# Local attention in a woven one-core kernel: first-pass exponentials kept and transposed, instead of scores and exponentials computed a second time

## What is computed

```python
sim = jnp.einsum('bhwid,bhwjd->bhwij', bq, bk)      # bq scaled by 8; keys: own window and the one before
mask = (i < j) | (i > j + WINDOW) | (j == -1)
sim = jnp.where(mask, -jnp.finfo(sim.dtype).max, sim)
attn = jax.nn.softmax(sim, axis=-1)
out = jnp.einsum('bhwij,bhwjd->bhwid', attn, bv)
```

## Time and profile before

| | |
|---|---|
| median of 3 runs | 2591.12 us (2587.27 to 2595.66) |
| the profiled execution | 2581.11 us |
| its span, first to last instruction | 2579.3 us |
| mean granted TensorE clock | 0.866 |
| instructions | 53778 |

### The profile page before, as it was taken

One profiled execution on the slowest core, in us unless ns is written; L12 is line 12 of the kernel. 1 busy time (PEld: TensorE's weight loads), 2 busy tenths in 40 slices (PEclk: granted clock), 3 DMA queues, 4 the chain that ended last, 5 costly groups with the idle time before them and its releaser, 6 DMA issues.

```text
span 2579.3 us, 53778 instructions
## 1 busy us (share of the span) xinstructions
PE 1943.3 (75%) x22054; PEld 1184.7 (46%) x22054; DVE 1351.0 (52%) x3132; ACT 1387.3 (54%) x3607; POOL 553.8 (21%) x613
## 2 busy tenths in 40 slices
PE   4239656888769777888779786888778876977777
PEld 3014344546444554446444454446444544456444
DVE  5133446554554737464654647374655556473553
ACT  1154525764476616763476527673476537672534
POOL 2710205030221105030312004030413023110230
PEclk9659867998889978998789878998799878997999
DMA  9203360002000100002000201002100201000000
GB/s 275 61 3 94 102 165 13 3 1 51 10 10 2 38 15 17 3 1 51 13 6 2 50 10 9 3 1 51 18 3 1 51 10 10 2 8 13 1 1 5
DMA packets 129890, 76.26 MB, mean 30 GB/s; under 512 B 76082, under 2 KB 121610, under 8 KB 127596
## 3 DMA queue, kind: packets, MB, share of 16 engines
q1 hardware_dynamic: 125548, 66.51, 10.6%
q0 software_dynamic: 4096, 6.32, 2.0%
HBM read 41.71 MB, written 33.16 MB: 29 GB/s over the span
## 4 chain that ended last, share of the span: by engine, by line
PE 38%; issue 23%; DVE 15%; ACT 12%; POOL 6%; another core or an unknown queue 3%; SPq 2%; DMA 1%; DVEq 0%; POOLq 0%; ACTq 0%
PE PS L1292 4%; PE PS L1433 4%; PE PS L596 3%; POOL area_b L1740 2%; DVE work_a L975 2%; PE PS L488 2%; ACT work_a L814 2%; PE PS L1325 2%; PE PS L1444 2%; PE PS L752 2%; PE PS L568 2%; DVE area_b L1625 2%; PE PS L1402 2%; PE PS L1364 1%
## 5 line engine op out<-in xcount | busy, mean ns | idle before, releaser
L1740 POOL TENSOR_TENSOR area_b<-area_b,tables 128x256 f32<-128x256 f32 x256 | 213.0, 852 | 761.7 <-DVE area_b L1625 761.7
L797 ACT ACTIVATE work_a<-PS,work_a 128x512 bf16<-128x512 f32 (+3 forms) x512 | 265.2, 543 | 132.7 <-DVE work_a L924 119.9
L924 DVE TENSOR_REDUCE work_a<-PS 128x2 f32<-128x1024 f32 (+3 forms) x256 | 201.4, 820 | 148.1 <-PE PS L488 86.5
L488 PE MATMUL PS<-strip,pick 64*128 64x128 bf16 (+4 forms) x2560 | 250.7, 277 | 0.0
L1529 ACT ACTIVATE area_b<-PS,neg_max 128x192 f32<-128x192 f32 (+1 forms) x512 | 202.3, 421 | 75.9 <-DVE neg_max L1665 58.6
L814 ACT ACTIVATE work_a<-PS 128x1024 f32<-128x1024 f32 (+1 forms) x192 | 169.4, 882 | 113.4 <-PE PS L488 112.9
L1292 PE MATMUL PS<-wqkv,area_b 128*128 128x512 f32 x384 | 201.9, 659 | 9.1 <-DVE area_b L1625 8.7
L534 PE MATMUL PS<-work_a 64*128 64x512 bf16 (+3 forms) x512 | 77.7, 345 | 159.1 <-ACT work_a L797 119.5
L1325 PE MATMUL PS<-area_b 64*128 64x192 f32 (+1 forms) x1024 | 141.6, 405 | 68.8 <-ACT area_b L1529 53.8
L596 PE MATMUL PS<-work_a 128*64 128x512 f32 (+3 forms) x1024 | 188.9, 471 | 4.0 <-ACT work_a L814 4.0
L1754 POOL TENSOR_TENSOR rstd_b<-var_eps_b,minus_half 128x4 f32<-128x4 f32 x16 | 16.4, 1025 | 786.5 <-DVE var_eps_b L120 786.5
(11 more groups left out here) (310 smaller groups left out, 4107.5 us busy)
## 6 DMA issues: line engine op xcount, KB each, us to landing
work_a<-stack_d SPq DMA_DIRECT2D x32, 512.0 KB
stack_d<-area_b SPq DMA_DIRECT2D x48, 192.0 KB, 3.3
stack_d<-area_b SPq DMA_DIRECT2D x32, 128.0 KB, 2.7
area_b<-in_L_attn_x_dram SPq DMA_DIRECT2D x4, 512.0 KB, 6.4
slots_in<-work_a SPq DMA_DIRECT2D x8, 256.0 KB, 4.9
stack_d<-work_a SPq DMA_DIRECT2D x4, 512.0 KB, 7.3
work_a<-xnT_d SPq DMA_DIRECT2D x8, 256.0 KB
work_a<-in_L_attn_x_dram SPq DMA_DIRECT2D x8, 256.0 KB
```

What stands on the lines that cost most here:

```text
L488: return nc.tensor.matmul(to, pick16[half_rows(e), half * P:(half + 1) * P], rows, start=False, stop=True, tile_position=(64 * e, 0), skip ...
L797: nc.scalar.activation(dump0[:, n % 2 * T:n % 2 * T + (i + 1) * P], PS[:, a:a + (i + 1) * P], ACT.Exp, bias=neg_max0[:, k:k + 1], accum_ou ...
L924: nc.vector.reduce_max(neg_max0[:, 2 * g * NT + i:(2 * g + 2) * NT:NT], at[:, :, Q_AT[i]:Q_AT[i] + (i + 1) * P], AX_X, negate=True).then_i ...
L1740: nc.gpsimd.tensor_tensor(to[:, n, :, r, :], src[:, n, :, 1 - r, :], table(2 * n + 1, t)[:, 32 * r:32 * r + 32].unsqueeze(1).to_broadcast( ...
```

## The change

It keeps the exponentials of the first pass in `work_b`, 896 columns for each head. DVE divides by the sums (`shared_out`: one reciprocal of 4 columns and four in-place products with a scalar for each partition, for each slot; slot m - 2 is handled behind the maximum of slot m, the last two at the first slot of the second pass). In the second pass PE transposes these blocks (8 f32 transposes of 128x128 in an even slot, 6 in an odd one), ACT copies them out with a plain copy of the same size as the former exponential, and the product with the values stays. The first 64 keys of a block that belong to the previous tile are taken with 64 columns of zeros before them; POOL writes these zeros (8 x 3 x 64 = 1536 columns) once for each layer, after waiting for the last `turned_q` and `turned_k`. PE's second pass waits for that and, for each pair of heads, for the products. Logarithms, shifts, their transposes and copies, the constant `select16` and the second pass of scores, masks and exponentials go. `probs2T` and the context now lie in `q2` and `k2`.

```diff
@@ -245,20 +243,16 @@
-probs2 = work_b[:, 0:2 * 768]
-dump2 = work_b[:, 2 * QK:3 * QK]
-ctx2T = rot
+probs2T = q2[:, 0:2 * 768]
+ctx2T = k2
...
-shiftT2 = sb("shiftT2", 2 * T, BF16)
...
-log_sums2 = sb("log_sums2", H2 * NT)
-shift_rest2 = sb("shift_rest2", NT * H2)
-shift_part2 = sb("shift_part2", NT * H2, BF16)
+inv_sums2 = sb("inv_sums2", H2 * NT)
@@ -446,6 +439,21 @@
+def probs_of(h, i):
+    a = h * 896 + (0, 192, 448, 704)[i]
+    return work_b[:, a:a + Q2_KEYS[i]]
...
+def own_keys_of(h, i):
+    return probs_of(h, i)[:, Q2_KEYS[i] - P:]
...
+def late_keys_of(h, i):
+    a = h * 896 + 256 * i - P
+    return work_b[:, a:a + P]
...
+zeros_of_probs2 = work_b.rearrange("p (h c) -> p h c", c=896)[:, :, P:].rearrange(
+    "p h (i c) -> p h i c", c=256)[:, :, :, 0:64]
@@ -1303,13 +1311,6 @@
-def shifts_T(half, k):
-    pe.wait_ge(s["shift_parts"], past("shift_parts", 3 * half + 3))
-    for i in range(NT):
-        a = (half * NT + i) * P
-        last = nc.tensor.transpose(bank(k, i * P, (i + 1) * P), shift_parts2[:, a:a + P], ident)
-    last.then_inc(s["shiftT"], 1)
@@ -1340,49 +1341,31 @@
     if m == 0:
-        fill(4)
+        fill(7)
         pe.wait_ge(s["sum"], past("sum", 28))
-        shifts_T(0, 4)
-        fill(3)
-        pe.wait_ge(s["shiftT_copied"], past("shiftT_copied", 1))
+        pe.wait_ge(s["zeroed"], past("zeroed", 1))
     else:
         pe.wait_ge(s["probs"], past("probs", m))
-    if m == 4:
-        pe.wait_ge(s["shiftT_copied"], past("shiftT_copied", 2))
-    half = g // 2
-    for j in (2 * x, 2 * x + 1):
-        n = K2_QUERIES[j]
-        for e in range(2):
-            h = 2 * g + e
+    pe.wait_ge(s["shared"], past("shared", 8 * g + 8))
+    for e in range(2):
+        for j in (2 * x, 2 * x + 1):
             a = (4 + e) * BANK + K2_AT[j]
-            nc.tensor.matmul(PS[:, a:a + n], select16[half_rows(e), (h % HH) * P:(h % HH + 1) * P],
-                             shiftT2[half_rows(e), half * T + j * P:half * T + j * P + n],
-                             start=(j % 2 == 0), stop=False, tile_position=(64 * e, 0),
-                             skip_group_check=True)
-        for e in range(2):
+            if j + 1 < NT:
+                nc.tensor.transpose(PS[:, a + P:a + 2 * P], late_keys_of(2 * g + e, j + 1), ident)
+            if j % 2:
+                nc.tensor.transpose(PS[:, a:a + P], own_keys_of(2 * g + e, j), ident)
+        for j in (2 * x, 2 * x + 1):
             a = (4 + e) * BANK + K2_AT[j]
-            nc.tensor.matmul(PS[:, a:a + n], k2[half_rows(e), g * T + j * P:g * T + (j + 1) * P],
-                             q2[half_rows(e), g * T + j * P:g * T + j * P + n], start=False, stop=False,
-                             tile_position=(64 * e, 0), skip_group_check=True)
-    for late in range(2):
-        for e in range(2):
-            to = bank(4 + e, 0, W2K[x])
-            if x:
-                last = limits(late, e, to, (2, 1)[late], 5)
-            else:
-                last = limits(late, e, to.rearrange("p (n c) -> p n c", c=KX), (2, 4)[late], 3, 2)
-    last.then_inc(s["scoresT"], 1)
+            if j % 2 == 0:
+                last = nc.tensor.transpose(PS[:, a:a + P], own_keys_of(2 * g + e, j), ident)
+    last.then_inc(s["flipped"], 1)
 if m == 1:
     pe.wait_ge(s["sum"], past("sum", 32))
-    shifts_T(1, 7)
 if m:
...
     pe.wait_ge(s["probs"], past("probs", m))
-    if x == 0:
-        if g == 1:
-            pe.wait_ge(s["shiftT_copied"], past("shiftT_copied", 2))
-        if g >= 2:
-            pe.wait_ge(s["ctxT"], past("ctxT", g - 1))
+    if x == 0 and g >= 2:
+        pe.wait_ge(s["ctxT"], past("ctxT", g - 1))
     for j in (2 * x, 2 * x + 1):
@@ -1390,7 +1373,7 @@
-last = nc.tensor.matmul(PS[r:r + D2, o:o + n], v2[:, v:v + D2], probs2[:, a:a + n],
+last = nc.tensor.matmul(PS[r:r + D2, o:o + n], v2[:, v:v + D2], probs2T[:, a:a + n],
@@ -1505,48 +1488,27 @@
-def shift_logs(half):
-    at = slice(half * NT * HH, (half + 1) * NT * HH)
-    act.wait_ge(s["sum"], past("sum", NT * HH * (half + 1)))
-    nc.scalar.activation(log_sums2[:, at], sums2[:, at], ACT.Ln).then_inc(s["log"], 1)
...
-def shifts_copied(half, k):
-    act.wait_ge(s["shiftT"], past("shiftT", half + 1))
-    nc.scalar.copy(shiftT2[:, half * T:(half + 1) * T], bank(k)).then_inc(s["shiftT_copied"], 1)
...
-n = 0
 for m in range(8):
     g, x = divmod(m, 2)
-    if m == 7:
-        shifts_copied(0, 4)
     act.wait_ge(s["max"], past("max", 3 * g + (2, 3)[x]))
...
             a, w = (4 + 2 * x + e) * BANK + Q2_AT[i], Q2_KEYS[i]
-            if n >= 4:
-                act.wait_ge(s["sum"], past("sum", n - 3))
-            nc.scalar.activation(dump2[:, n % 4 * 256:n % 4 * 256 + w], PS[:, a:a + w], ACT.Exp,
+            nc.scalar.activation(probs_of(2 * g + e, i), PS[:, a:a + w], ACT.Exp,
                                  bias=neg_max2[:, k:k + 1], accum_out=sums2[:, k:k + 1]
                                  ).then_inc(s["sum"], 1)
-            n += 1
-    if m == 3:
-        shift_logs(0)
-    if m == 7:
-        shift_logs(1)
     yield
...
         x = m % 2
-        act.wait_ge(s["scoresT"], past("scoresT", m + 1))
+        act.wait_ge(s["flipped"], past("flipped", m + 1))
         if m >= 2:
...
         a = 768 * (m % 2)
-        nc.scalar.activation(probs2[:, a:a + 2 * W2K[x]].rearrange("p (e c) -> p e c", e=2),
-                             PS[:, 4 * BANK:6 * BANK].rearrange("p (e c) -> p e c", e=2)[:, :, 0:W2K[x]],
-                             ACT.Exp).then_inc(s["probs"], 1)
-    if m == 1:
-        shifts_copied(1, 7)
+        nc.scalar.copy(probs2T[:, a:a + 2 * W2K[x]].rearrange("p (e c) -> p e c", e=2),
+                       PS[:, 4 * BANK:6 * BANK].rearrange("p (e c) -> p e c", e=2)[:, :, 0:W2K[x]]
+                       ).then_inc(s["probs"], 1)
     yield
@@ -1633,27 +1595,18 @@
-def shifts(half):
-    at = slice(half * NT * HH, (half + 1) * NT * HH)
-    to = shift_parts2[:, half * NT * P:(half + 1) * NT * P].rearrange("p (i e c) -> p i e c", e=2, c=64)
-    dve.wait_ge(s["log"], past("log", half + 1))
-    nc.vector.scalar_tensor_tensor(
-        shift_rest2[:, at].rearrange("p (i h) -> p h i", h=HH),
-        log_sums2[:, at].rearrange("p (h i) -> p h i", i=NT), -1.0,
-        neg_max2[:, at].rearrange("p (h i) -> p h i", i=NT),
-        ALU.mult, ALU.add).then_inc(s["shift_rest"], 1)
-    rest_, part = shift_rest2[:, at], shift_part2[:, at]
-    for n in range(3):
-        dve.wait_ge(s["shift_rest"], past("shift_rest", 3 * half + n + 1))
-        if n:
-            dve.wait_ge(s["shift_parts"], past("shift_parts", 3 * half + n))
-        nc.vector.tensor_copy(part, rest_).then_inc(s["shift_part"], 1)
-        dve.wait_ge(s["shift_part"], past("shift_part", 3 * half + n + 1))
-        nc.vector.tensor_copy(to[:, :, :, n * HH:(n + 1) * HH],
-                              part.rearrange("p (i h) -> p i h", h=HH).unsqueeze(2).to_broadcast(
-                                  [P, NT, 2, HH])).then_inc(s["shift_parts"], 1)
-        if n < 2:
-            nc.vector.tensor_tensor(rest_, rest_, part, ALU.subtract).then_inc(s["shift_rest"], 1)
+def shared_out(m):
+    g, x = divmod(m, 2)
+    sums, inv = (buf[:, 2 * g * NT:(2 * g + 2) * NT].rearrange("p (e i) -> p e i", e=2)[:, :, 2 * x:2 * x + 2]
+                 for buf in (sums2, inv_sums2))
+    dve.wait_ge(s["sum"], past("sum", 4 * m + 4))
+    nc.vector.reciprocal(inv, sums).then_inc(s["inv_sum"], 1)
+    dve.wait_ge(s["inv_sum"], past("inv_sum", m + 1))
+    for i in (2 * x, 2 * x + 1):
+        for e in range(2):
+            k = (2 * g + e) * NT + i
+            nc.vector.tensor_scalar(probs_of(2 * g + e, i), probs_of(2 * g + e, i), inv_sums2[:, k:k + 1], None,
+                                    ALU.mult).then_inc(s["shared"], 1)
@@ -1667,14 +1620,13 @@
                          negate=True).then_inc(s["max"], 1)
-if m == 4:
-    dve.wait_ge(s["max"], past("max", 6))
-    shifts(0)
+if m >= 2:
+    shared_out(m - 2)
 yield
...
 if m == 0:
-    dve.wait_ge(s["max"], past("max", 12))
-    shifts(1)
+    shared_out(6)
+    shared_out(7)
 if m and m % 2 == 0:
@@ -1748,6 +1700,9 @@
+gp.wait_ge(s["turned_q"], past("turned_q", NT))
+gp.wait_ge(s["turned_k"], past("turned_k", NT))
+nc.gpsimd.memset(zeros_of_probs2, 0.0).then_inc(s["zeroed"], 1)
@@ -2161,9 +2116,6 @@
-nc.vector.tensor_copy(select16[:, :].rearrange("p (h d) -> p h d", d=P),
-                      head(C_SEL, HH).unsqueeze(2).to_broadcast([P, HH, P]))
-nc.vector.memset(shift_parts2[:, :], 0.0)
```

9 lines of the change are left out of this document (3 added, 6 removed).

## The result

The kernel before took 2583.90 us in the median of 8 runs (2577.15 to 2595.66), the changed one 2603.23 us (2593.41 to 2610.69): a ratio of 1.0070, 95% interval 1.0045 to 1.0094, 18 us slower. Timed again on another occasion the ratio was 1.0073 (1.0046 to 1.0100). The prediction's range of 2560 to 2621 holds the time, and "slower" had the largest of its three chances (0.38). But its sum was +2 us, no change, and the change costs 18; the measured 2603 lies outside the 2583 to 2599 that it gave for that case.

The account below looks back on a forecast made before the run. No engine is full throughout; the last wait in each stage bounds it (ACT full in layer 0, DVE and DMA ending layer 1). 7 x (0.9 + 0.4) - 7 = +2 us on 2591 gives 2593 us, no change; range 2560 to 2621.

Parts of the forecast that it names:

- The step that failed: POOL in layer 1: nothing needed soon is queued behind its wait and zeros; no cost was counted.
- The products in the convolution chain: Layer 1's first pass: products enter DVE's convolution chain, which has 0.17 us of idle time; +1.0 us a batch.
- Layer 0: Seven times beside A: gather +1.8, product collisions +0.5, ACT's relief -1.4; together +0.9 us a batch.
- The link of DVE's return to the gather's end: Layer 0, slot 2: DVE returns from its stall about 1.1 us after POOL's last gather instruction.
- the half that I took for the gather: Layer 0: gather moves 3.5 us later; half, +1.8 us a batch, taken for DVE's return, between 0 and 3.5.
- line 1002 starts some 0.4 us later: Layer 1: the last two products replace shifts and partly fit into idle time, delaying the inverse and line 681 too.
- line 681's idle time swallows the second pass's gain: End of layer 1: second pass ends about 2.7 us earlier; PE's idle time grows from 2.63 to over 5 us.
- The last batch: B alone, PE slots on the path: -3.5 us a layer, -7 in all, between -9 and -3.
- The start: DVE's preparations for select16 and shift_parts2 go, before a long wait for other work: 0 us.
- The gather: Rival, slower: POOL's wait and zeros push layer 0's gather, DVE returns only behind it; 2605 us, 2621 with slow zeros; chance 0.27.
- Relief pays: Rival, faster: layer 0's stall does not follow the gather, products hide in DVE's idle time; -24, 2567 us; chance 0.32.
- The clock: Rival, slower: transposes in PE's second pass fail to hold the clock, a pair takes 7.1 us; +88, 2679 us; chance 0.11.

Follow-up runs that it names:

- before_zeros: Kernel before, with only POOL's two waits and a memset of 1536 columns added where the change has them; 2605.86 us, ratio 1.0076.
- product_later: Changed kernel with slot 0's reciprocal and products in layer 1 moved from slot 2 to slot 3, behind the convolution; 2593.98 us, ratio 1.0040.
- no_products2: Changed kernel without DVE's 32 products of a layer (values unscaled; reciprocals, zeros and waits stay); 2514.77 us, ratio 1.0056, second chip.
- best1: Changed kernel, zeros behind gather (layer 0) and rstd_a (layer 1), layer 1's products of slots 0 to 2 behind slot 3; 2583.59 us, ratio 1.0001.
- combined2: Changed kernel, zeros behind gather and rstd_a, layer 1's products of slots 0 to 2 behind slot 3, next batch's loads late; 2513.16 us, ratio 1.0053.
- rstd_first2: Changed kernel with POOL's zeros of layer 1 moved behind A's rstd_a, layer 0's left in place; 2511.16 us, ratio 1.0042, second chip.
- zeros_late: Changed kernel with POOL's turned_k wait and zeros moved later in B's first pass, both layers; in layer 1 still ahead of rstd_a; 2603.47 us, ratio 1.0063.
- best2: Changed kernel with zeros behind gather and rstd_a, and layer 1's products of slots 0 to 3 made by POOL; 2588.75 us, ratio 1.0015.
- loads_late2: Changed kernel with SP's loads for the next batch issued behind the inverse's DMA round trip instead of ahead; 2547.35 us, ratio 1.0195, second chip.
- after_again: The changed kernel itself, unaltered, timed and profiled once more; 2603.69 us, ratio 1.0073.

## The prediction against the runs, step by step

**The step that failed** is one sentence of the POOL part: "In layer 1 nothing is queued behind POOL that is needed soon." A's `rstd_a` is, and DVE waits for it within a microsecond of the statistics. The prediction asked of POOL what the gather of layer 0 would do, and did not list POOL's next instructions in layer 1. Price by the rows: 10.6 us for the wait itself (1.45 in six batches, 1.91 in one), and some 5 more between line 1143 and line 970, which come without any product (before_zeros 6.3, product_later 5.1, no_products2 5.9) and are gone where `rstd_a` is on time and the products too (best1, combined2: 0.0). The 5 stand mostly in DVE's longer waits for B's scores. Together some 16 us in the rows. The medians bear out the cause better than this size: the wait and zeros alone cost the kernel before 20 us, both layers together; taking them from in front of `rstd_a` alone gave 7 us, with 0 to 14 allowed.

**The products in the convolution chain:** predicted 1.0 a batch, measured 0.8 (5.8 us in rstd_first2 with nothing else in that row, 5.5 by product_later). Right. A product takes 0.313 us on average, a slot's four 0.94 to 1.02 with their overlap and the reciprocal 0.2: 1.2, as taken. The zeros took 1.38 us; 1.4 was taken.

**Layer 0:** +0.9 a batch predicted, +1.3 measured. The parts are not those predicted. The link of DVE's return to the gather's end holds in three batches of seven (1.3 us behind it), and the gather starts 3 to 6 us later against line 681 in six of the seven; but zeros_late, with the gather back, was no faster, so the half that I took for the gather was too much. What fills the +1.3 instead stays open. no_products2 against rstd_first2 speaks for the products (9.7 us); before_zeros speaks against them, with +8.8 in layer 0 and no product; and the row itself varies by 6.6 us between best1 and best2.

**Line 1002 and the end of layer 1:** "line 1002 starts some 0.4 us later" is 0.6 us earlier against the convolution, which was to start 1.0 later; it starts 0.7 us earlier (-5.1 in the table). Right. That line 681's idle time swallows the second pass's gain is right, and larger than said: 7.61 us of idle time in the batch shown, 6.9 on average of the seven, where over 5 were forecast. The second pass itself came out as worked out: 3.64 us a pair against 3.8.

**The DMA step** was not in the prediction: 4.8 us. loads_late2 shows the collision (the step falls to 2.6 or 2.7 us without the loads), and that it does not pay to move them. Why the loads come nearer to the store is argued only. They follow the low triangle's trip, the store follows line 1002, and between line 995 and line 1002 the change saves 1.5 us a batch, where the last shifts and the wait ahead of them stood. The products are not the reason: no_products2 has none, its loads are issued 8.6 to 8.9 us ahead of the store, and its row is +6.1.

**The last batch:** -7 predicted, -7.9 measured, and -4.5 in after_again. Right within what a second profile changes. **The start:** 0 predicted, -2.3 in this execution and +0.7 in after_again's, so nothing.

**The rivals.** "The gather" (2605) has the number by luck: its reason is refuted by zeros_late; what is true of it is that POOL's wait and zeros carry the loss (before_zeros), and by the rows mainly in the other layer. "Relief pays" fell: the gain of PE and ACT was there and had no place where it counted, but in the last batch. "The clock" fell: from 1186 to 1196 the granted clock was 1.00, the upper of its levels, with 14 of the 30 instructions of a pair of slots transposes, and it was 1.00 in every second pass of layer 1 and of the last batch. Over the whole span it is lower after, 0.839 against 0.866: 0.72 against 0.79 in the head, 0.91 against 0.98 between line 1002 and line 681, where PE now idles longer, and 0.85 against 0.865 in layer 0, where ACT is the bound. best1 has 0.845 and the time of the kernel before. The Trainium skill (TensorE: Matmul & The Clock Gate, Part 4: PE-mode transpose) would have transposes not count as activity; with products with the values between them every microsecond or so this trace does not show the clock fall, and no run here had transposes alone.

**What was luck.** Taking the failed step in, the sum would have been +2 + 16 = +18, or 2609 on 2591, beside a ratio of 1.0070 that gives 2609. That agreement is partly luck: it leaves out 3 us in layer 0 and the 4.8 us of the DMA step, and of these some 5 are made up for by the start, the last batch and the products, which came out a little cheaper than forecast. So is the small distance of 10 us between 2593 and 2603: the 2591 under the sum is the median of three runs, 7 us above the 2583.90 of all eight. And the range held the time because it reached up to two wrong reasons for "slower".

## What to carry to other kernels

A wait that is added to an in-order engine has to be priced in every stage and every layer in which it stands, by listing the next instructions on that engine and who waits for each; a 1 us step of another stream queued behind it can cost more than the new arithmetic beside it (by the rows of layer 1, some 16 us against 5.5). Work that nobody needs until later (here the zeros) goes behind such steps, and new work on a chain goes where the engine idles already: best1 took back 20 us with nothing but such moves. And an edit of an order is a test only if the trace shows that the order changed; a row that is read from one profile needs a second one of the same kernel beside it.
